# Early wide blocks of sweep 1 grouped by column 0 alone, then columns 1 and 2, 3 and 4, and so on

## The reference

```python
h = relu(layernorm(x));  y = h
for k in range(2):                                   # sweeps 1 and 2
    y = tanh(concatenate([adj @ y, y], 1) @ W0[k])
x = x + y
h = relu(layernorm(x));  x = x + adj @ (h @ W1) + bias            # sweep 3
h = relu(layernorm(x));  x = x + adj @ (h * (u >= 0.1) / 0.9)     # sweep 4
h = relu(layernorm(x))                                            # sweep 5
x = x + concatenate([h, adj @ h / (rowsum(adj) + 1)], 1) @ W3.T
```

## Time and profile before

| | us |
|---|---|
| median of three runs | 2417.26 |
| lowest, highest | 2416.97, 2418.13 |
| profiled execution | 2418.83 |
| its span | 2415.8 |
| TensorE busy in the span | 2366.0 |
| VectorE busy in the span | 1009.7 |

### The profile page before, as it was taken

One profiled execution on the slowest core, in us unless ns is written; L12 is line 12 of the kernel. 1 busy time (PEld: TensorE's weight loads), 2 busy tenths in 40 slices (PEclk: granted clock), 3 DMA queues, 4 the chain that ended last, 5 costly groups with the idle time before them and its releaser, 6 DMA issues.

```text
span 2415.8 us, 24269 instructions
## 1 busy us (share of the span) xinstructions
PE 2366.0 (98%) x9920; PEld 1183.3 (49%) x9920; DVE 1009.7 (42%) x2073; ACT 141.5 (6%) x315; POOL 13.4 (1%) x23
## 2 busy tenths in 40 slices
PE   5999999999999999999999999999999999999998
PEld 3544545454455444444454444444444544444665
DVE  6855546555453211100078787876411110005211
ACT  1000000000001311100010000000000000000000
POOL 0000000000000000000000000000000000000000
PEclk9999999999999999999999999999999999999999
DMA  9999999999997788888868888886899999999998
GB/s 386 421 416 352 370 355 364 353 363 347 361 365 287 276 285 292 298 294 301 339 258 341 295 301 301 311 317 261 310 376 370 360 374 355 361 374 370 357 422 351
DMA packets 118638, 820.88 MB, mean 340 GB/s; under 512 B 14593, under 2 KB 18817, under 8 KB 19329
## 3 DMA queue, kind: packets, MB, share of 16 engines
q1 hardware_dynamic: 113904, 814.79, 88.2%
q10 hardware_dynamic: 3856, 2.46, 0.3%
q0 software_dynamic: 768, 2.10, 0.3%
HBM read 817.20 MB, written 2.10 MB: 339 GB/s over the span
## 4 chain that ended last, share of the span: by engine, by line
PE 93%; DMA 5%; DVE 1%; issue 0%; ACTq 0%; ACT 0%; POOL 0%; DVEq 0%; SPq 0%; POOLq 0%
PE double_acc L591 56%; PE spare L591 12%; PE single_acc L567 12%; PE spare L567 8%; DMA ring<-in_adj 5%; PE natural L637 2%; PE spare L653 1%; PE spare L615 1%; PE natural L641 1%; DMA ones_sb<-in_ones 1%; DVE centred L750 0%; DVE stats L738 0%; DVE deg_part L780 0%; DVE deg_part L779 0%; DVE moments L741 0%
## 5 line engine op out<-in xcount | busy, mean ns | idle before, releaser
L591 PE MATMUL double_acc<-ring,operand 128*128 128x512 f32 x3144 | 1371.7, 594 | 2.9 <-DVE operand L890 1.3
L591 PEld LDWEIGHTS double_acc<-ring,operand 128*128 128x128 f32 x3144 | 589.1, 190 | 720.3 <-issue 713.1
L567 PE MATMUL single_acc<-ring,operand 128*64 128x256 f32 x3008 | 355.4, 385 | 39.1 <-DMA ones_sb<-in_ones 21.6
L819 DVE TENSOR_TENSOR sums<-double_acc,sums 64x256 f32<-64x256 f32 x120 | 50.7, 422 | 752.5 <-PE double_acc L591 751.6
L591 PE MATMUL spare<-ring,operand 128*128 128x512 f32 x672 | 298.9, 597 | 0.0
L567 PEld LDWEIGHTS single_acc<-ring,operand 128*64 128x64 f32 x3008 | 205.5, 137 | 185.5 <-issue 36.8
L780 DVE TENSOR_TENSOR deg_part<-deg_part,ring 128x1024 f32<-128x1024 f32 x214 | 262.1, 1225 | 7.3
L779 DVE TENSOR_TENSOR deg_part<-deg_part,ring 128x1024 f32<-128x1024 f32 x214 | 261.9, 1224 | 7.3 <-DMA ring<-in_adj 0.9
L792 DVE TENSOR_TENSOR partial<-spare,partial 64x256 f32<-64x256 f32 (+1 forms) x190 | 80.4, 423 | 290.6 <-PE spare L591 144.6
L591 PEld LDWEIGHTS spare<-ring,operand 128*128 128x128 f32 x672 | 124.3, 190 | 152.2 <-issue 152.2
L567 PE MATMUL spare<-ring,operand 128*64 128x256 f32 x1456 | 163.5, 381 | 0.7 <-DVE partial L792 0.7
(11 more groups left out here) (54 smaller groups left out, 583.3 us busy)
## 6 DMA issues: line engine op xcount, KB each, us to landing
ring<-in_adj SPq DMA_DIRECT2D x756, 1024.0 KB, 6.7
held<-in_adj SPq DMA_DIRECT2D x17, 1024.0 KB, 8.8
resid<-in_x SPq DMA_DIRECT2D x16, 128.0 KB, 10.2
kept<-in_adj SPq DMA_DIRECT2D x2, 1024.0 KB, 9.7
for_layer<-in_u POOLq DMA_DIRECT2D x16, 128.0 KB, 2.4
out_rows<-for_layer ACTq DMA_DIRECT2D x16, 128.0 KB, 6.9
w_both_sb<-in_w_both ACTq DMA_DIRECT2D x2, 80.0 KB, 7.9
w_own_sb<-in_w_own ACTq DMA_DIRECT2D x2, 32.0 KB, 8.9
```

What stands on the lines that cost most here:

```text
L567: last = nc.tensor.matmul(acc[half_of(h), 0:HALF], operand[:, b.j * TPB + t, half_of(b.row.half)], stream[:, t, nodes_of(h)], start=b.firs ...
L591: last = nc.tensor.matmul(acc[:, :], operand[:, b.j * TPB + t, :], stream[:, t, :], start=b.first and t == 0, stop=b.last and t == TPB - 1)
L819: last = nc.vector.tensor_tensor(to, got[own, nodes_of(h)], to, ALU.add)
```

## The change

The early blocks of sweep 1 are grouped by other columns. Before, the columns are taken in pairs 0 and 1, 2 and 3, and so on, and the pair 2m, 2m+1 is worked off in rows 2m+2 and 2m+3. Now column 0 stands alone and is worked off in rows 1 and 2, columns 1 and 2 in rows 3 and 4, columns 3 and 4 in rows 5 and 6, and so on. The rule for `double` follows it: of odd rows two blocks and of even rows three are left to the row itself (row 1 has d(1,0), row 2 d(2,0) and d(2,1)); before it was the other way round.

```diff
-        self.double = {1: [*range(max(0, (i - 2) // 2 * 2), i)], 2: [*range(NB - 1, i, -1)], 3: [*range(i)], 4: [*range(NB - 1, i, -1)]}\
+        self.double = {1: [*range(max(0, (i - 1) // 2 * 2 - 1), i)], 2: [*range(NB - 1, i, -1)], 3: [*range(i)], 4: [*range(NB - 1, i, -1)]}\
...
     for row in ROWS[:NB]:
-        m = (row.i - 2) // 2
-        below = [*range(2 * m + 4, NB)] if m >= 0 else []
+        m = (row.i - 1) // 2
+        columns = [j for j in (2 * m - 1, 2 * m) if j >= 0]
+        below = [*range(2 * m + 3, NB)] if m >= 0 else []
         half = len(below) // 2
-        mine = below[:half] if row.i % 2 == 0 else below[half:]
-        start = 4 if row.i % 2 == 0 else 1
+        mine = below[:half] if row.i % 2 else below[half:]
+        start = 4 if row.i % 2 else 1
...
-                early(mine[given], [2 * m, 2 * m + 1])
+                early(mine[given], columns)
```

## The result

| | before | changed kernel |
|---|---|---|
| median, us | 2417.47 (12 runs, 2416.26 to 2418.51) | 2411.73 (12 runs, 2411.10 to 2414.56) |
| ratio | | 0.9977, 95% interval 0.9969 to 0.9985 |
| profiled execution: time, span | 2418.83, 2415.8 | 2411.64, 2409.8 |
| start of block 1,2 | 56.09 | 55.98 |
| end of d(1,0) | 97.09 | 112.10 |

The changed kernel is 5.7 us faster. 4.83 were forecast, 2412.4 against 2411.73 measured.

A forecast was written before the change was run, and what follows sets the result against it. Row 1 was taken as bound by DMA, later rows by TensorE. +15.44 us up to d(1,0) and -20.27 behind it sum to -4.83, giving 2412.4 us from the median 2417.26; range 2410.9 to 2414.8.

The forecast's parts named there:

- What bounds row 1: Row 1 of sweep 1: bound by DMA, one block landing every 2.48 us at 421 GB/s, before and after.
- Up to the end of d(1,0): Sweep 1 up to d(1,0): six more loads at the landing pace make it end 15.44 us later, at 112.53.
- the start of (8,0): Last of six wide blocks moved into row 1: starts at 103.36 us, five loads after the block at 90.85.
- Behind it: Sweep 1 after d(1,0): six fewer wide blocks, one more narrow run, -20.27 us if TensorE never waits.
- Row 2 never waits: Row 2 of sweep 1: 50.6 us of work against 52.1 of landings, the lead covers it, no TensorE wait.
- The rival of a DMA-bound row 2: Slots freed late slow landings and row 2 waits: gain only 3.0 us or 1 to 2, 2413.6 to 2417; chance 0.21.
- the lead of 3.7 us: Start of row 2: block 2,3 lands at 110.7 and is wanted at 114.4; 2.2 us left after row 2.
- VectorE's later additions cost nothing: Row 1: slots freed 5.4 us after landing, up to 3.4 before; loads still issued 14.4 us ahead, cost nothing.
- Mixing costs 0.34 us a run: Sweep 1: leaving narrow blocks costs TensorE 0.19 us and entering them 0.15, 0.34 for each run.
- The rival by which mixing costs nothing: No price for switching between wide and narrow blocks: -5.75 us, 2411.5, or 2410.9 with slightly faster landings; chance 0.13.
- The end of the sweep: Row 15 of sweep 1: VectorE has 3.4 us less ahead of its last sums; costs nothing, the post's wait stays.
- the bound of 0.2%: Whole kernel: measurement can tell about 0.2%, 4.8 us, from no change; the forecast gain stands just on that line.

The follow-up runs named there:

- dose0: Changed kernel with all 13 wide blocks of column 0 in row 2 and none in row 1, new column groups kept; 2418.72 us, ratio 1.0006.
- before_by3: Kernel before the change, with its early groups three together from row 3 on, 67 narrow runs instead of 84; 2410.82 us, ratio 0.9974.
- dose13: Changed kernel with all 13 wide blocks of column 0 in row 1 and none in row 2; 2411.03 us, ratio 0.9974.
- ring5: Changed kernel with a ring of five slots instead of eight, profiled once; 2439.46 us.
- after_by3: Changed kernel with early groups three together from row 3 on, 73 narrow runs instead of 90; 2405.86 us, ratio 0.9950.
- after_tpd: Changed kernel with post and degree sums directly on the turn from row 2 on, 73 narrow runs instead of 90; 2406.48 us, ratio 0.9954.
- best6: Changed kernel with groups three together and turn, post and degree sums together, 51 narrow runs instead of 90; 2397.93 us, ratio 0.9919.
- the second series: The changed kernel measured once more, unchanged, against new runs of the kernel before; 2412.08 us, ratio 0.9978.

## Why the prediction was right, point by point

- *What bounds row 1*: right. Six wide blocks, 20.6 us of TensorE's work, went in for 15.1 us of time, and the landings kept their 2.48 us and 421 GB/s.
- *Up to the end of d(1,0)*: +15.44 us forecast. Measured from the start of 1,2: 56.12 us (again 56.16) against 41.00, so +15.12. The step that is off is the start of (8,0), 46.91 us behind 1,2 and not 47.27. The forecast hung this on block 1,1 of a single execution, 90.85 - 56.09 = 34.76 us behind 1,2. dose0, whose row 1 is the same, has 90.19 - 55.66 = 34.53 there, and before_by3 90.42 - 55.65 = 34.77. So up to 0.2 of the 0.3 us can be such a difference; what the rest is stays open. The size of this step was off, not its mechanism.
- *Behind it*: -20.27 us forecast. Measured from the end of d(1,0) to the post: 641.80 us, in both executions, against 759.15 - 97.09 = 662.06, so -20.26. Six wide blocks and one narrow run account for all of it.
- *Row 2 never waits*: right, 63.50 of 63.50 us busy. The rival of a DMA-bound row 2 didn't come: the lead of 3.7 us was enough, and dose13 shows that it may be spent on 14 narrow blocks where it is larger. ring5 shows that the rival was a real one: with a ring of five, slots freed late do hold loads back in row 2.
- *VectorE's later additions cost nothing*: right, with 16.6 us from issue to landing where 14.4 was worked out. The working took 2 us off the cover (a slot freed 5.4 us after its landing and not 3.4), and 18.8 became 16.1 us. ring5 shows that three slots fewer begin to matter, by 1.0 us in row 1 and 1.9 behind it.
- *Mixing costs 0.34 us a run*: right and a little low, 0.35 to 0.37 in four kernels. The rival by which mixing costs nothing gave -5.75, which is close to the measured median of -5.7, but it isn't the cause: before_by3, after_by3, after_tpd and best6 all show the price. Of the 5.7, sweep 1 is 5.14; the rest is differences between executions as far as is known, and the second series has 5.0. By the median alone the first series lies just outside the forecast's own span of 4.3 to 5.3 us and next to that rival; it is the stretches, not the median, that tell the two apart. That the median came so near the rival is chance.
- *The end of the sweep*: right, the post waits 0.94 us as before.
- *Against the bound of 0.2%*: the forecast stood on it, and the measured ratio of 0.9977 is just beyond, with an interval that reaches back to 0.9985.

## What to carry to other kernels

Where a stretch is bound by transfers, work that costs the engine more than its transfer costs the DMA is paid there only with the time of its transfer; its worth is engine time minus transfer time for each piece, and it ends when the waiting is filled (six pieces gave 6.8 us, seven more 1.1). Count the changes between kinds of matmul as well as the matmuls: here the order alone, with the same 9920 records of matmuls, was worth another 13.8 us, more than twice the change itself. Check the lead that the following stretch lives on, not only its average.

## What was not expected

- The price of entering and leaving a run of narrow (128 x 64 weights) matmuls is 0.35 to 0.37 us, whether wide matmuls, the small products of a post or degree sums of one column interrupt it. (For the transposes of a turn in sweep 1 only the entering behind them is seen, 1.88 us; they never stand without a narrow block ahead.) No wait shows it, for the trace counts it as busy: TensorE's busy time is 2365.2 us in the changed kernel and 2350.9 in best6, for the same matmuls. In the chain it is 7.06 against 6.87 and 1.88 against 1.73 us. The chain's sum of 0.34 is a little less than the 0.35 to 0.37 measured; what the difference is was not pursued.
- Slow loads in row 0 are passed on to the end. In dose13's profiled execution 1,2 began at 57.77 us (others with eight slots 55.65 to 56.26) and its span was 2411.1, although its sweep 1 was 1.12 us shorter than the changed kernel's. From 22 to 30 us the DMA moved 358 GB/s in that execution, and 413 in the changed kernel's. Its runs spread from 2409.64 to 2412.91 us. Whether the kernel before would take up such a late start in its waits of row 1 is not shown: there the loads themselves set the pace, and here they were the late ones.
